# Splitting the normalisation of a joined projection into other pieces and on other engines

## The reference, cut to what matters

```
x = x + _L0_attn_ref(_layernorm(x), ...)       # then .. @ Wo
x = x + _L0_xattn_ref(_layernorm(x), ctx, ...)
x = x + _L0_ffn_ref(_layernorm(x), ...)
x = x + _L1_attn_ref(_layernorm(x), ...)       # then .. @ Wo + bo
x = x + _L1_xattn_ref(_layernorm(x), ctx, ...) # then .. @ Wo.T + bo
x = x + _L1_ffn_ref(_layernorm(x), ...)        # routed experts
```

## Time and profile before

| | us |
|---|---|
| median of three runs | 1452.22 |
| lowest and highest | 1447.64, 1460.55 |
| the profiled execution, its own time | 1442.37 |
| span of the profiled execution | 1440.6 |
| TensorE busy | 1225.4 (85%) |
| VectorE busy | 790.5 (55%) |
| ScalarE busy | 773.1 (54%) |
| GpSimd busy | 353.4 (25%) |

### The profile page before, as it was taken

One profiled execution on the slowest core, in us unless ns is written; L12 is line 12 of the kernel. 1 busy time (PEld: TensorE's weight loads), 2 busy tenths in 40 slices (PEclk: granted clock), 3 DMA queues, 4 the chain that ended last, 5 costly groups with the idle time before them and its releaser, 6 DMA issues. The chain is left out here.

```text
span 1440.6 us, 25459 instructions
## 1 busy us (share of the span) xinstructions
PE 1225.4 (85%) x8789; PEld 727.6 (51%) x8790; DVE 790.5 (55%) x1717; ACT 773.1 (54%) x1480; POOL 353.4 (25%) x585
## 2 busy tenths in 40 slices
PE   4959999999999978888446899888884799999992
PEld 2313444434434345445115563454452799999991
DVE  5878777777777516334787644563346322222223
ACT  3726777777777763464586667534643233333330
POOL 1832222222222212134520000141133222222220
PEclk9958999999999999999668999999996799999996
DMA  6680203312221011000001000132046111111115
GB/s 214 210 261 20 71 25 90 67 44 70 68 73 41 3 32 66 1 1 5 19 0 35 1 2 1 37 132 110 2 136 195 30 37 36 36 36 37 36 30 182
DMA packets 58656, 89.86 MB, mean 62 GB/s; under 512 B 10329, under 2 KB 48371, under 8 KB 56883
## 3 DMA queue, kind: packets, MB, share of 16 engines
q1 hardware_dynamic: 52694, 76.19, 17.6%
q0 software_dynamic: 3744, 10.23, 2.3%
q10 hardware_dynamic: 2112, 2.10, 0.4%
HBM read 66.21 MB, written 21.89 MB: 61 GB/s over the span
## 5 line engine op out<-in xcount | busy, mean ns | idle before, releaser
L999 DVE CUSTOM_DVE_ANT_0 faded_scores_sb<-banks,inner_sb 128x1024 f32<-128x1024 f32 x256 | 303.3, 1222 | 92.1 <-PE banks L838 90.9
L1098 ACT ACTIVATE xt_sb<-banks 128x512 f32<-128x512 f32 x344 | 179.0, 605 | 71.9 <-PE banks L845 71.8
L845 PE MATMUL banks<-q_stack_sb,k_stack_sb 99*128 99x128 bf16 (+3 forms) x960 | 180.5, 297 | 5.9 <-ACT xt_sb L1098 2.6
L838 PE MATMUL banks<-k_stack_sb,q_stack_sb 96*128 96x512 bf16 (+3 forms) x704 | 163.2, 338 | 7.1 <-DVE peak_sb L999 4.0
L845 PEld LDWEIGHTS banks<-q_stack_sb,k_stack_sb 99*128 99x128 bf16 x960 | 70.4, 97 | 159.6 <-ACT xt_sb L1098 66.6
L2300 PEld LDWEIGHTS banks<-slots_xt_sb,attn_sb 128*128 128x128 f32 x1248 | 147.6, 195 | 1.9
L2300 PE MATMUL banks<-slots_xt_sb,attn_sb 128*128 128x128 f32 x1248 | 147.8, 278 | 0.0
L2312 PE MATMUL banks<-experts_w_sb,xt_sb 128*128 x624 | 141.3, 380 | 1.3 <-issue 1.3
L2312 PEld LDWEIGHTS banks<-experts_w_sb,xt_sb 128*128 128x128 f32 x624 | 115.7, 190 | 15.6 <-issue 1.7
L2352 ACT ACTIVATE slots_xt_sb<-banks 128x256 f32<-128x256 f32 x39 | 14.9, 383 | 176.1 <-PE banks L2286 176.1
L2409 DVE TENSOR_TENSOR slots_y_sb<-banks,tile_b_sb 128x256 f32<-128x256 f32 x39 | 16.6, 425 | 166.6 <-PE banks L2312 166.6
(11 more groups left out here) (334 smaller groups left out, 2051.5 us busy)
## 6 DMA issues: line engine op xcount, KB each, us to landing
experts_w_sb<-in_L_ffn_W SPq DMA_DIRECT2D x16, 1024.0 KB, 12.1
k_stack_sb<-k_parts SPq DMA_DIRECT2D x48, 256.0 KB, 4.7
q_stack_sb<-q_parts SPq DMA_DIRECT2D x96, 128.0 KB, 3.4
q_parts<-parts_sb SPq DMA_DIRECT2D x16, 384.0 KB, 2.5
k_parts<-parts_sb SPq DMA_DIRECT2D x16, 384.0 KB, 3.4
xt_sb<-outputs_y SPq DMA_DIRECT2D x8, 512.0 KB, 5.9
x_sb<-in_x SPq DMA_DIRECT2D x4, 512.0 KB, 5.5
w_raw_sb<-in_w_t SPq DMA_DIRECT2D x2, 1024.0 KB, 7.1
```

Of the source, the lines that this page charges most:

```text
L838: last = pe.matmul(k.ps[:, 2 * (tile % 2) + half, lo - half * G:hi - half * G], stacks.q[0:ROWS, g % 3, version, h, j * P:(j + 1) * P], st ...
L845: return pe.matmul(k.ps[:, bank, at:at + hi - lo], stacks.k[0:ROWS + PARTS, g // 2 % 2, version, h, kt * P:(kt + 1) * P], stacks.q[0:ROWS ...
L999: dve.tensor_tensor_reduce(out=junk[:, tile % 2, :], in0=tile_scores(tile), in1=inner[:, window(tile)], scale=1.0, scalar=-3.0e38, op0=ALU ...
L1098: act.activation(out, k.ps[:, bank_of((exp_done, u + 1)), :], ACT.Exp).then_inc(exp_done, 1)
```

## The change

`project_normalise` alone is changed. The first piece is tiles 0 to 7, and all eight are normalised by ScalarE. Of the second piece, tiles 8 to 12 are normalised by VectorE and tiles 13 to 15 by ScalarE. GpSimd normalises none. `scale(0)` now stands between the adds of tiles 9 and 10. The turned groups go to banks 0 and 1, 2 and 3, 4 and 5, 6 and 7, so the copy of an earlier group is not waited for, but groups 2 and 3 wait until all tiles were added. ScalarE's order is: eight tiles, copies of group 0, `root(1)`, copies of group 1, three tiles, copies of groups 2 and 3.

```diff
-    FIRST = 3 * TPG
+    FIRST = 2 * TPG
+    LAST_BY_ACT = 3
...
+        ACT_TILES = [t for t in range(NT) if t < FIRST or t >= NT - LAST_BY_ACT]
+
+        def turned_bank(g, kd):
+            return 2 * g + kd
...
-            pool.wait_ge(turned, NG)
-            pool.wait_ge(scaled, 1)
-            for t in range(NT):
-                if by_pool(t):
-                    pool.tensor_scalar(attn[:, t, :], k.x[:, t, :], mv[:, t, 0:1], rstd[:, t:t + 1],
-                                       ALU.subtract, ALU.mult).then_inc(xn_by_pool, 1)
...
             def turn_normalised(g):
-                pe.wait_ge(at_done, KD * (3 + g % 2))
-                wait(pe, xt_done, KD * (g - 1))
+                if g < 2:
+                    pe.wait_ge(at_done, KD * (3 + g))
+                else:
+                    pe.wait_ge(added, NT)
                 for t in range(g * TPG, (g + 1) * TPG):
-                    if by_act(t):
-                        pe.wait_ge(xn_by_act, t // 2 + 1)
-                    elif by_pool(t):
-                        pe.wait_ge(xn_by_pool, t // 2 + 1)
+                    if t in ACT_TILES:
+                        pe.wait_ge(xn_by_act, ACT_TILES.index(t) + 1)
                     else:
                         pe.wait_ge(xn_by_dve, t - FIRST + 1)
                     for kd in range(KD):
                         j = t % TPG
-                        last = pe.transpose(k.ps[:, 2 * (g % 2) + kd, j * P:(j + 1) * P],
+                        last = pe.transpose(k.ps[:, turned_bank(g, kd), j * P:(j + 1) * P],
...
             root(0)
+            def normalise_tile(t):
+                act.activation(attn[:, t, :], k.x[:, t, :], ACT.Identity, bias=shift[:, t:t + 1],
+                               scale=rstd[:, t:t + 1]).then_inc(xn_by_act, 1)
+
             act.wait_ge(scaled, 1)
-            for t in range(NT):
-                if by_act(t):
-                    act.activation(attn[:, t, :], k.x[:, t, :], ACT.Identity, bias=shift[:, t:t + 1],
-                                   scale=rstd[:, t:t + 1]).then_inc(xn_by_act, 1)
+            for t in range(FIRST):
+                normalise_tile(t)
+            copy_turned(0)
             root(1)
-            for g in range(NG):
-                copy_turned(g)
+            copy_turned(1)
+            act.wait_ge(scaled, 2)
+            for t in range(NT - LAST_BY_ACT, NT):
+                normalise_tile(t)
+            copy_turned(2)
+            copy_turned(3)
...
-            for t in range(FIRST, NT):
+            for t in range(FIRST, NT - LAST_BY_ACT):
                 dve.tensor_scalar(attn[:, t, :], k.x[:, t, :], mv[:, t, 0:1], rstd[:, t:t + 1],
                                   ALU.subtract, ALU.mult).then_inc(xn_by_dve, 1)
```

More of the change, by code:

```diff
@@ L309, in project_normalise @@
         k.sem("dve_own"), k.sem("table_own"), k.sem("var_ready"), k.sem("std_ready"), k.sem("scaled"))
-    xn_by_act, xn_by_pool, xn_by_dve = k.sem("xn_by_act"), k.sem("xn_by_pool"), k.sem("xn_by_dve")
+    xn_by_act, xn_by_dve = k.sem("xn_by_act"), k.sem("xn_by_dve")
     xn_turned, xt_done = k.sem("xn_turned"), k.sem("xt_done")
-    FIRST = 3 * TPG
+    FIRST = 2 * TPG
+    LAST_BY_ACT = 3
     PIECES = [(0, FIRST), (FIRST, NT)]
@@ L412, in copy_turned @@
                 for kd in range(KD):
-                    act.activation(k.xt[:, kd, g * G:(g + 1) * G], k.ps[:, 2 * (g % 2) + kd, :], ACT.Copy).then_inc(xt_done, 1)
+                    act.activation(k.xt[:, kd, g * G:(g + 1) * G], k.ps[:, turned_bank(g, kd), :], ACT.Copy).then_inc(xt_done, 1)
             root(0)
+            def normalise_tile(t):
+                act.activation(attn[:, t, :], k.x[:, t, :], ACT.Identity, bias=shift[:, t:t + 1],
+                               scale=rstd[:, t:t + 1]).then_inc(xn_by_act, 1)
             act.wait_ge(scaled, 1)
-            for t in range(NT):
-                if by_act(t):
-                    act.activation(attn[:, t, :], k.x[:, t, :], ACT.Identity, bias=shift[:, t:t + 1],
-                                   scale=rstd[:, t:t + 1]).then_inc(xn_by_act, 1)
+            for t in range(FIRST):
+                normalise_tile(t)
+            copy_turned(0)
             root(1)
-            for g in range(NG):
-                copy_turned(g)
+            copy_turned(1)
[4 more added lines that the diff above has]
+            copy_turned(3)
         @block.vector
```

## The result

| | before | after |
|---|---|---|
| median of 8 runs each, us | 1452.18 | 1439.38 |
| lowest and highest | 1447.64, 1460.55 | 1434.27, 1451.51 |
| profiled execution, us | 1442.37 | 1434.35 |
| its span | 1440.6 | 1432.6 |

The ratio of the run times is 0.9935 with a 95% interval of 0.9911 to 0.9959, so about 9.4 us less (6.0 to 12.9). The forecast was 9.7, and as a time 1442.5 where the median came at 1439.4; the two medians differ by 12.8, at the far end of that interval. The spans of the two profiled executions differ by 8.0.

A forecast was written before the change was run, and what follows sets the result against it. Each joined block's tail was bound by the chain through GpSimd's six tiles, not TensorE. Gains of 3.3 + 3.3 + 3.1 = 9.7 us off the 1452.2 median gave 1442.5, range 1432 to 1453.

The forecast's parts named there:

- The first piece is earlier: Joined block: needs tile 7's statistics, not tile 11's; first tile at 547.85, ScalarE's eight take 4.06 us, hidden behind the projection.
- The second root loses nothing behind the copies: ScalarE: copies of group 0 end and the second variance is ready both at about 553.0, so the order costs nothing.
- VectorE's five tiles: Second piece: five tiles instead of four take 2.2 us, until 556.5; 2.04 if VectorE is freed of GpSimd.
- The clock: TensorE, group 3's eight transposes: 1.04 us high, 1.8 low; taken low, low, high, gains 3.3, 3.3, 3.1.
- The margin of 0.3 us: Tile 10's add, delayed by `scale(0)`, ends at 548.2, before tile 14's matmul due at 548.45; costed at nothing.
- Eight banks: Turned groups in eight banks cost and bring nothing; with four, copies would end before the tiles arrive.
- SyncE's cover in the third block: Expert weights issue until 1086.94 and the block can't end before; new end 1089.6 leaves 2.7 us of cover.
- A: Clock helps: both cross-attention blocks are spared the 1.2 GHz stretch about 20 us in; gain 14.5, 1437.7 us; 13%.
- B: Clock hurts: two cross-attention starts run at half rate, 9.1 us more each; 8.5 slower, 1460.7 us; 5%.
- C: Tail not shortened as said, ScalarE late everywhere: gain 5.7 at most or down to 3, 1446.5 to 1449 us; 12%.
- its bound for held matmuls: Projection matmuls held by adds delayed by the moved `scale(0)`: at most 0.5 us a block.

The follow-up runs named there:

- the two runs with one edit each: Kernel before with first piece of eight tiles instead of twelve: closing stretches 8.6, then 7.9 us less; or with GpSimd's six tiles given to ScalarE: 2.4 us longer.
- the piece of eight: Kernel before with the first piece eight tiles instead of twelve, all else kept; closing stretches sum 48.73 and 49.48 us in two profiles, ratio 0.995.
- The early bias: Changed kernel with the two output biases loaded a block earlier; closing stretches 16.05, 16.35, 16.21 us, sum 48.61, 0.95 less than the changed kernel.

## Why the prediction was right, point by point

Times here are counted from the start of the closing stretch, which was 543.26 in the prediction and is 540.87 in the profile after.

**The first piece is earlier: right.** First tile predicted at 4.59, measured 4.55. Eight tiles predicted 4.06 us, measured 4.04. That it is this, and not GpSimd's removal, that carries the gain was the prediction's chain, and the two runs with one edit each show it: 8.6 and 7.9 us less in two profiles of the one, 2.4 more for the other.

**The second root loses nothing behind the copies: right.** Predicted at 9.7, measured 9.71; ScalarE waited 0.16 for VectorE.

**VectorE's five tiles: mis-sized, 2.2 us predicted, 1.70 measured.** I kept the rate that the rows showed with GpSimd beside it. Without, each took 407 to 411 ns, as in the normalisation blocks; started every 0.32 they give 1.70, even less than the 2.04 I had named as the lower figure, which left out that they overlap. It didn't matter, as the run with all eight on VectorE shows.

**The clock: right for two blocks, wrong for the third.** I took high there, by the 0.89 of the old stretch, and it fell as in the others. The sum was said to be 9.0 with the low clock in all three, and that would have been the better forecast. A point of the argument was too short as well: the prediction had only group 3 priced at the low clock, behind the last tile. In truth the low stretch covers most of all 16 transposes, and they fall behind the tiles from the start. The fault in VectorE's price and this one cancelled, which is luck: the transposes' end was predicted at 15.0 and came at 15.02. Nor is the clock in the third block fixed: in the second profile of the piece of eight it stayed at 1.00 there, and the last 16 transposes took 2.61.

**The margin of 0.3 us: wrong in the second and third block.** "A margin of 0.3: I cost it at nothing" is the step that failed. The adds' schedule was right, but the variance before them was stretched by 0.5 and 0.3 us. The prediction looked for GpSimd and VectorE meeting only where something was taken away, at the normalised tiles. The earlier piece moves the variance from behind GpSimd's bias adds to beside them: before, they ended at 942.8 and the variance began at 945.77. The early bias shows it: variance 0.17 again, wait gone.

The third block accounts for most of the miss: predicted 3.1, measured 1.77. Of the 1.3 missing, 0.75 is the clock as priced there and 0.17 the stretched matmuls. Its 16 transposes took 3.60, where those of the first took 3.35, and they started 4.78 behind the matmuls' end instead of 4.60. In the second block the 0.56 missing is 0.38 of stretched matmuls and the same 0.18.

**Eight banks: worth nothing in the closing stretch, shown** by the run with four.

**SyncE's cover in the third block: held.** The expert weights' last issue ended at 1082.86, 4.1 before the block's end at 1086.93.

**The rivals.** A didn't come: the low stretch about 20 us into cross-attention is still there (0.51 from 577 to 582). B didn't come in the changed kernel: the first 10 us behind the joined blocks are at 1.00. But its mechanism is real: in 6 of 12 places of kernels with the early piece and the idle pause cross-attention did start low, and its first three lines lost 1.4 to 1.5 us in five of them and 2.1 in one, instead of the 9.1 it was priced at: the clock was up again 2.9 to 4.3 us behind their start. Its one profile doesn't tell how often the changed kernel itself pays this. C fell: ScalarE's tiles overlap as before, and only its bound for held matmuls came, in part.

Against the medians: closing stretches say 7.8, the runs 9.4 with an interval from 6.0. The forecast of 9.7 is within it, 1.9 above what the rows add up to.

## What to carry to other kernels

When a list of waits names a slow engine, ask what its first item waits for: here the earlier start of the piece was worth 7.9 to 8.6 us, and relieving the slow engine alone cost 2.4, because its work went in front of something else in another engine's order. When a step is moved earlier, look up what other engines do in its new place, for its own duration too. A short phase in which TensorE has little to do cost twice here, as a pause and as a low clock behind it, and spare work in the pause was a cheap repair.

## What the runs showed of the hardware

**VectorE held up by GpSimd.** The variance, a VectorE TENSOR_SCALAR of 0.17 us (read and write in SBUF, 128 x 8), was begun while GpSimd was at its last bias adds in 14 places of all profiles. In each it ended 0.02 to 0.06 us after the last of these adds: in three places its 0.17 just reached that far, in the other 11 it took 0.19 to 1.13. In three of these 11 (0.97, 0.96 and 1.13) it had begun in the last add but one and stood through the last as well: GpSimd's next add went ahead of it. VectorE's statistics beside the same adds kept their 0.42, and its eight aggregations their 0.64. VectorE's adds that read a PSUM bank and one SBUF tile took 0.42 beside the same GpSimd adds, as without them. The Trainium skill, "SBUF — State Buffer", section "SBUF: two separate sides", has the two share a port pair that goes to one of them for its whole instruction. The ends agree with it. That the variance stood through a second add as well is not in that sentence, and no run here looks at the port itself.

**The clock behind a pause.** In the changed kernel TensorE's clock was at 1.2 GHz for most of the last 16 transposes behind a pause of 2.6 us, in each of three blocks (granted clock 0.59, 0.57, 0.53). With 16 more transposes in the pause they ran at 2.4 (1.00 in all three). The pause doesn't bring the low clock every time: in the third block of the second profile of the piece of eight, pauses of 0.55 and 1.71 us were followed by 1.00. In kernels with the early piece the next block started at 1.2 in 6 of 12 places without such work and in none of six with it. The Trainium skill, "TensorE: Matmul & The Clock Gate", section "What's actually happening", has idleness lower this clock, and the runs with and without work in the pause agree.

**The spread of run times goes with the clock.** The spans of the changed kernel's eight runs against their mean granted clock: 1432.6 at 0.924, 1432.5 and 1436.3 at 0.922, 1434.0 at 0.921, 1439.0 at 0.920, 1442.4 at 0.916, 1447.3 at 0.911, 1449.7 at 0.910. A line through all eight falls by 1.2 us for each 0.001. In the two profiles compared here most of the difference lies in one block. The last 86 us of the second cross-attention in the changed kernel, and the same instructions in 93 us with the last eight all on VectorE, whose code there is the same:

```profile
975.00:1061.00 86.00, 75.20 (x642) 35.41 (x642) 27.24 (x53) 50.10 (x61) 9.17 (x44) 0.95 0.04 13
```

```profile
975.00:1068.00 93.00, 82.35 (x640) 37.95 (x636) 27.34 (x53) 50.51 (x61) 9.25 (x44) 0.87 0.03 11
```

What makes a run fall into the one or the other is open. For a change of half a per cent it means that a single run time says little, and that the stretch touched has to be read by itself.
